# Which signal lets SyncE reload the down weights in the expert stage of a routed layer

## What is computed

```python
    capacity = max(1, int(N / E * K * CAP_FACTOR))        # 640 for N = 4096, E = 32, K = 4
    ...
    buf = jnp.zeros((E + 1, capacity, d), xf.dtype).at[e_s, p_s].set(xf[tok])[:E]
    h = jax.nn.silu(jnp.einsum('ecd,edh->ech', buf, wg)) * jnp.einsum('ecd,edh->ech', buf, wu)
    out_e = jnp.einsum('ech,ehd->ecd', h, wd)
    gathered = out_e[flat_e, jnp.minimum(pos, capacity - 1)]
    contrib = gathered * (flat_g * keep.astype(xf.dtype))[:, None]
    routed = jnp.zeros_like(xf).at[tok].add(contrib)
    return (shared + routed).reshape(b, s, d)
```

## Time and profile before

| | |
|---|---|
| runs | 621.44, 623.31, 626.21 us; median 623.31 us |
| profiled execution | span 719.4 us; the page gives no other time for it |
| busy over the span | TensorE 573.4 us (80%), VectorE 418.4 (58%), GpSimd 350.9 (49%), ScalarE 322.5 (45%) |
| down projection, line 1148 | 640 records, 293 ns mean, 85.3 us busy |
| result copies, line 812 | 160, 372 ns mean, 44.7 us busy, 122.8 us idle ahead of them |
| scatter of results, line 625 | 160, 976 ns mean, 156.2 us busy, 135.0 us idle ahead of them |
| loads of down weights, line 328 | 32 of 128 KB |

### The profile page before, as it was taken

One profiled execution on the slowest core, in us unless ns is written; L12 is line 12 of the kernel. 1 busy time (PEld: TensorE's weight loads), 2 busy tenths in 40 slices (PEclk: granted clock), 3 DMA queues, 4 the chain that ended last, 5 costly groups with the idle time before them and its releaser, 6 DMA issues.

```text
span 719.4 us, 20830 instructions
## 1 busy us (share of the span) xinstructions
PE 573.4 (80%) x7427; PEld 459.8 (64%) x7427; DVE 418.4 (58%) x1281; ACT 322.5 (45%) x832; POOL 350.9 (49%) x394
## 2 busy tenths in 40 slices
PE   4578988788778888675758798888888888798685
PEld 2346756556555556454535688888888888788553
DVE  5766778587777777553435555444445554454155
ACT  4255756455665655443433243334444433343310
POOL 8210143555555554555567045555555555655610
PEclk9579999899999999987679898999999999999998
DMA  7899888566666444300000233322334334332069
GB/s 249 235 242 241 246 229 259 152 204 199 175 188 192 133 113 106 73 18 18 9 10 8 73 117 122 96 85 83 114 99 119 116 112 129 119 104 77 17 246 343
DMA packets 79417, 98.33 MB, mean 137 GB/s; under 512 B 12097, under 2 KB 59999, under 8 KB 79216
## 3 DMA queue, kind: packets, MB, share of 16 engines
q1 hardware_dynamic: 65280, 82.92, 39.5%
q0 software_dynamic: 9216, 12.02, 5.4%
q10 hardware_dynamic: 4848, 2.40, 1.1%
HBM read 50.00 MB, written 54.30 MB: 145 GB/s over the span
## 4 chain that ended last, share of the span: by engine, by line
PE 35%; another core or an unknown queue 13%; issue 11%; ACT 11%; SPq 8%; DMA 7%; POOL 7%; DVE 5%; ACTq 1%; POOLq 1%; DVEq 0%
PE banks L1122 9%; PE banks L1148 7%; SPq L352 4%; ACT yout L812 4%; PE banks L939 3%; DMA rload<-pair_results 3%; DMA rotated_keys<-parts 3%; POOL expert_slots L491 3%; ACT hact L793 2%; SPq L393 2%; PE banks L889 2%; PE banks L920 2%; ACT pt L662 2%; DVE mx L1246 2%
## 5 line engine op out<-in xcount | busy, mean ns | idle before, releaser
L625 POOL DMA_INDIRECT pair_results<-yout,yidx x160 | 156.2, 976 | 135.0 <-ACT yout L812 91.8
L491 POOL DMA_INDIRECT expert_slots<-xfe,sidx x128 | 128.3, 1002 | 133.3 <-issue 51.9
L1122 PE MATMUL banks<-xgT_parts,wgu_parts 128*128 128x320 f32 x768 | 149.1, 347 | 29.2 <-ACT hact L793 29.2
L1122 PEld LDWEIGHTS banks<-xgT_parts,wgu_parts 128*128 128x128 f32 x768 | 126.9, 209 | 40.5 <-ACT hact L793 33.1
L1508 DVE TENSOR_TENSOR hact<-hact,banks 128x320 f32<-128x320 f32 x128 | 57.0, 482 | 130.5 <-ACT hact L793 119.3
L662 ACT ACTIVATE pt<-banks 128x512 f32<-128x512 f32 x128 | 69.5, 595 | 78.9 <-PE banks L920 53.3
L1246 DVE TENSOR_REDUCE mx<-banks 128x8 f32<-128x1024 f32 x64 | 78.2, 1222 | 45.2 <-PE banks L889 43.5
L812 ACT ACTIVATE yout<-banks,ypair 128x128 f32<-128x128 f32 x160 | 44.7, 372 | 122.8 <-remote 61.8
L1148 PE MATMUL banks<-wdn,hact 128*128 128x128 f32 x640 | 85.3, 293 | 2.7 <-DVE hact L1508 1.7
L1148 PEld LDWEIGHTS banks<-wdn,hact 128*128 128x128 f32 x640 | 85.1, 212 | 3.1 <-issue 3.1
L793 ACT ACTIVATE hact<-banks 128x320 f32<-128x320 f32 x128 | 53.4, 452 | 48.6 <-PE banks L1122 30.0
(11 more groups left out here) (155 smaller groups left out, 945.8 us busy)
## 6 DMA issues: line engine op xcount, KB each, us to landing
expert_slots<-xg SPq DMA_DIRECT2D x32, 325.0 KB, 4.7
xg<-expert_slots SPq DMA_DIRECT2D x32, 325.0 KB
pair_results<-zero SPq DMA_DIRECT2D x32, 256.0 KB
rload<-pair_results SPq DMA_DIRECT2D x16, 512.0 KB, 9.5
kS<-rotated_keys SPq DMA_DIRECT2D x32, 240.0 KB
qS<-rotated_queries SPq DMA_DIRECT2D x32, 192.0 KB
wgu<-in_L_ffn_wg_dram SPq DMA_DIRECT2D x32, 128.0 KB
wgu<-in_L_ffn_wu_dram SPq DMA_DIRECT2D x32, 128.0 KB
```

What stands on the lines that cost most here:

```text
L491: g.indirect_dma_start(out=slots_d, out_offset=bass.IndirectOffsetOnAxis(ap=sidx[:, m % NB, j, k:k + 1], axis=0), in_=xfe[:, m % NB, j, k, ...
L625: g.indirect_dma_start(out=pairs_d, out_offset=bass.IndirectOffsetOnAxis(ap=yidx[:, c, j:j + 1], axis=0), in_=yout[:, c, j, :], in_offset= ...
L1122: last = mm(bank[2 + 2 * w + h][:, 0:CH], wgu_parts[:, e.b, wp, w, h * P:(h + 1) * P], xgT_parts[:, e.b, xp, ch * CH:(ch + 1) * CH], start ...
```

## The change

SyncE's wait in `reload_down` names another semaphore. Before, the reload of expert e's down weights waits until the down projections of experts 0 to e - 2 are done (TensorE, `down_done`). After, it waits until the five copies of the results of each of them are done (ScalarE, `y_evac`, counted in fives). Nothing else changes: the load, its buffer, its place in SyncE's list and its own semaphore stay.

```diff
             def reload_down(e, c):
 
-                sp.wait_ge(S.down_done, e - 1)
+                sp.wait_ge(S.y_evac, ST * (e - 1))
                 load_wdn(e, c)
```

## The result

The kernel after takes 616.9 us (median of 18 runs, 610.96 to 620.67), the kernel before in the same rounds 621.71 us (18 runs, 613.83 to 626.21). The ratio is 0.9943, 95% interval 0.9915 to 0.9972: 3.5 us faster (1.7 to 5.3 on 621.71). It compares only runs within 1.5% of the fastest of their kernel, so it is not the quotient of the two medians, which lie 4.8 us apart. Of the 6.4 us between 623.3 and 616.9, 1.6 us come from the median of before, which is 621.71 over 18 runs and not the 623.31 of the first three.

What follows compares the result with a forecast made beforehand. The prediction saw the expert stage (265 of 719.4 us) bound by a chain of waits between engines, none of them full. Its terms summed to 30 x 0 = 0 us, so 623.3 us, range 618.5 to 628.1 us.

Steps and rivals of the forecast that it cites:

- The wait that goes, the wait that comes: SyncE ahead of the down weights' reload: issue moves from the down projection's end to the copies' end, 1.49 us later, 30 times.
- Who waits for the late load: TensorE's down projection two experts on: 11.0 us from issue to use, 5.4 us landing, 5.6 us left, so no wait.
- What is queued behind on SyncE: Slots' reload and gate/up weights: not held later, as one issue fits the 1.41 us gap with some 0.6 us left.
- Rival 1, slots late: Slots' load ahead of the transposes lands up to 1.26 us late, 30 times: up to 38 us slower, 661 us; chance 0.08.
- What the load now lies beside … I cost that at nothing: DMA queues: the load meets the first scatter and nears the slots' load; cost nothing, as DMA engines are at 0.35.
- Rival 2: VectorE's wait for a scatter's landing: scatters land sooner, 0.66 us per expert, 20 us faster, 603.5 us; chance 0.06.
- The pace: Expert stage: two experts take 17.1 us, 8.57 us each, and the round stays so after the change.
- Waits on scatters in many steps: Sign in the profile after that would prove the prediction wrong; the profile before showed one such wait, 0.66 us.

Runs made afterwards that it cites:

- f2: The kernel before without the 30 reloads of the down weights, so experts 2 to 31 use those of the first two: ratio 1.0001 to before, median 618.64 us.
- g1: The kernel before plus a spare 128 KB load per expert, issued when the five result copies are done: ratio 0.9960 to before, median 615.37 us.
- f3: The kernel before with six small VectorE copies into unused tiles behind line 1514, the load left where it was: ratio 0.9949 to before, median 620.12 us.
- e0: The kernel before, unchanged, run and traced again against itself: ratio 1.0001, median 623.69 us.
- g3: The kernel before, unchanged, one more trace only: 618.84 us in one run, no ratio.
- e1: The kernel after, unchanged, run again against the kernel before: ratio 0.9943, median 618.94 us.
- g4: The kernel after, unchanged, one more trace only: 616.74 us in one run, no ratio.

## Why the prediction was right and wrong

- *The wait that goes, the wait that comes*: right. 30 of 30 reloads wait for line 812, each 1.47 us later (1.49 forecast). The wait of 138 us was sized on the 719.4 us execution; it is 102.3. The slots' wait came out as forecast (33.4, "some 30").
- *Who waits for the late load*: right. In the kernel after TensorE's matmuls of line 1148 waited for no DMA, and f2, which has no such load, is no faster. The load's own landing, taken as 5.4 us, stands in no list of these runs either. The 2.3 us named beside it come from a fit that the Trainium skill, DMA: Bandwidth & Descriptors, section Anatomy of one DMA, gives for transfers issued by GpSimd; this load is issued by SyncE.
- *What is queued behind on SyncE*: right. The slots go out 0.24 us after `ypair`, and SyncE's waits sum to the same.
- *Rival 1, slots late*: did not happen. It needed a landing over some 4.3 us; the row shows 2.9.
- *"What the load now lies beside … I cost that at nothing"*: this is the step that failed. The bounds set beside it were 1.26 us of delay for the slots and 0.66 us of relief for VectorE; a later landing of the scatter had no place in them. What the load touched was the landing of a scatter, later by 0.58 us (2.69 against 2.11). Rival 2 looked at that landing and at the right wait but with the sign reversed: it asked for sooner landings, and priced them per expert (20 us). The gain comes from later ones, through an offset on another pair of engines that the text did not consider, and only where stalls stood: about 3.75 us between the traces, 3.5 us by the ratio. That the gain stayed within 1% was luck: no term of the sum held it down.
- *The pace*: the round was forecast at 17.1 us for two experts and is 12.73 us. The text noted that the runs are 96 us shorter and then read the spare time of TensorE, GpSimd and the scatters from that longer execution. At 6.365 us per expert GpSimd has no spare time, so an extra 0.3 to 0.5 us on a piece is kept; at 8.57 us, where GpSimd idles 135.0 us ahead of its pieces, it would have been absorbed (an argument, not a run), and the earlier trace rows is the only place where this could be guessed. "Waits on scatters in many steps" was named as what would prove the prediction wrong. They are there, but in before too (14 and 19 steps in its two later traces).

Shown: the collision and its price by offset (in all traces), the later landing beside a load (g1), that the load's absence keeps the collisions and the stalls (f2), that a shift of the split alone takes the stalls away (f3, in one trace and with an interval that only just misses 1). Also shown is that it takes the split: over all 14 traces some 800 pieces start within 0.35 us behind an instruction of lines 1508, 1523 or 1526, which read at most one input from SBUF, and each took 0.97 to 0.99 us (442.37 above, 0.10 us behind line 1526). Only argued: that a shared port is what lengthens the piece; no run varied the split's own operands.

## What to carry to other kernels

When a profiled execution's span is far from the runs' times, take no engine's spare time from it: the question "who has slack" gets its answer from the timed pace. Where two engines run at almost the same period, as GpSimd at 6.39 and TensorE at 6.365 us here, a small delay on the one was not hidden but collected, and a few tenths of a microsecond of phase decided whether the sum surfaced as a stall of several. A wait that gets longer can be the gain, so look at what it pushes out of whose way.

## What the runs showed of the hardware

A GpSimd scatter piece of 128 rows (0.97 us) is lengthened when it starts 0.03 to 0.5 us behind the start of VectorE's 128x512 `tensor_tensor` with both inputs in SBUF (0.68 us): it then ends 1.52 to 1.54 us after that start, so it takes up to 1.51 us. A piece that starts ahead of it keeps 0.97 us, and VectorE's instruction keeps its 0.68 us. Only where the two start within some 0.03 us of each other and the piece keeps its time does VectorE's take longer, up to 0.76 us (e0, 454.46). The Trainium skill, SBUF — State Buffer, section Who interferes with whom, says that a VectorE instruction with two SBUF inputs contends with a GpSimd instruction that reads SBUF, and that the order of issue decides which of them is blocked. The traces agree on both. The same section reports a `tensor_tensor` that did not hold up a DMA's descriptors; here the GpSimd instruction that issues an indirect scatter took up to 0.53 us longer, and whether it was held up in reading or in writing is not shown.

A scatter's last piece landed 2.1 to 2.4 us after its start with no load of down weights beside it (f2) or with that load of 128 KB issued a microsecond or more ahead of it (e0, g3; one landing of 2.53 us stands just behind a stall), 2.5 to 3.1 us with such a load 0.2 to 0.5 us behind it (e1; 2.69 and 2.71 us in g4 and g1), and 3.6 to 4.0 us when the slots' load (325 KB) and the gate and up weights went out from 0.4 to 0.6 us behind it on (e0, g3, f2, the first trace of after). In the last but one step landings of 4.2 to 4.5 us stand in three traces without a load of slots; why, no run shows.
